# Two attention layers on one core: the order of the work inside a slot, and projections one half per slot

## The reference, cut to what matters

```python
def layer0(x, mask, Wq, Wk, Wv, b):      # batch 8, width 256, 512 tokens, 16 heads of 16
    Q, K, V = (proj(W) for W in (Wq, Wk, Wv))
    att = einsum('bhqd,bhkd->bhqk', Q, K) * (1/4) + b[0]
    att = softmax(att * m + (1 - m) * -1e30, axis=-1)          # m: mask of the keys
    return einsum('bhqk,bhkd->bhqd', att, V), heads joined, transposed
def layer1(x, mask, Wq, Wo):             # 8 heads of 32; queries, keys and values are one projection
    q = xT @ Wq.T
    logits = (scale * q q^T * cmask + (1 - cmask) * -1e30) * rmask
    return (softmax(logits) @ q) @ Wo.T
x = x + layer0(x, cond_2048, ...)
x = x + layer1(x, cond_2048, ...)
x = x + GRU over 128 pairs of steps(cond_2048, x, ...)          # sequential
x = x + last layer(x, ...)
```

## Time and profile before

| | us |
|---|---|
| median of three runs | 2702.07 |
| lowest, highest | 2670.57, 2702.7 |
| the profiled execution's own time | 2684.75 |
| its span, first to last instruction | 2682.5 |
| tensor engine busy (matmuls) | 2099.1, 78% of the span |
| vector engine busy | 1187.9, 44% |
| scalar engine busy | 921.4, 34% |
| pool engine busy | 363.5, 14% |

### The profile page before, as it was taken

One profiled execution on the slowest core, in us unless ns is written; L12 is line 12 of the kernel. 1 busy time (PEld: TensorE's weight loads), 2 busy tenths in 40 slices (PEclk: granted clock), 3 DMA queues, 4 the chain that ended last, 5 costly groups with the idle time before them and its releaser, 6 DMA issues. The chain is left out here.

```text
span 2682.5 us, 89590 instructions
## 1 busy us (share of the span) xinstructions
PE 2099.1 (78%) x37964; PEld 1264.7 (47%) x37964; DVE 1187.9 (44%) x3349; ACT 921.4 (34%) x1836; POOL 363.5 (14%) x996
## 2 busy tenths in 40 slices
PE   4788888888989888967799777777777777777744
PEld 1233333333333433333344666666666666666631
DVE  3455454544445454413001444444444444444456
ACT  0534453434344343432122333333333333333313
POOL 0011111020111111010000111111111111111102
PEclk7889998988898888587899999999999999999967
DMA  7215151505041331211100000000000000000011
GB/s 189 72 59 147 42 137 36 138 27 143 25 134 48 93 81 34 59 55 37 84 0 1 0 0 0 0 0 0 0 0 0 0 0 0 0 0 0 0 36 63
DMA packets 53677, 116.79 MB, mean 44 GB/s; under 512 B 11302, under 2 KB 12198, under 8 KB 49886
## 3 DMA queue, kind: packets, MB, share of 16 engines
q1 hardware_dynamic: 50534, 115.03, 15.3%
q0 software_dynamic: 3072, 0.82, 0.2%
HBM read 77.16 MB, written 37.85 MB: 43 GB/s over the span
## 5 line engine op out<-in xcount | busy, mean ns | idle before, releaser
L789 PE MATMUL gate<-whh,hT 128*8 128x128 f32 x24576 | 718.6, 273 | 136.3 <-POOL xT L687 95.9
L789 PEld LDWEIGHTS gate<-whh,hT 128*8 128x8 f32 x24576 | 644.8, 90 | 168.9 <-POOL xT L687 112.1
L369 DVE TENSOR_REDUCE mx<-MX 128x1 f32<-128x512 f32 x768 | 497.5, 687 | 436.6 <-PE MX L507 434.6
L437 ACT ACTIVATE pr<-ST 128x1024 f32<-128x1024 f32 x384 | 390.2, 1024 | 373.3 <-PE ST L526 372.8
L507 PE MATMUL MX<-K,Q 51*128 51x512 f32 (+1 forms) x768 | 337.8, 558 | 98.0 <-DMA Q<-d_rows 40.9
L751 ACT ACTIVATE act<-pre 128x32 f32<-128x32 f32 x512 | 117.4, 229 | 725.4 <-DVE pre L710 465.8
L507 PEld LDWEIGHTS MX<-K,Q 51*128 51x128 f32 (+1 forms) x768 | 136.2, 215 | 407.3 <-DVE mx L369 205.3
L708 DVE STREAM_TRANSPOSE trn<-gate 128x128 f32<-128x128 f32 x256 | 81.2, 317 | 526.5 <-PE gate L789 526.5
L526 PE MATMUL ST<-Q,K 53*128 53x512 f32 (+1 forms) x768 | 256.6, 510 | 5.4 <-DMA Q<-nmp 4.6
L780 PE MATMUL gate<-identz,giz 128*8 128x32 f32 x8192 | 107.5, 193 | 141.6 <-issue 140.4
L767 PE MATMUL pg<-xT,wih 128*128 128x512 f32 x384 | 167.0, 598 | 19.1 <-DMA identz<-in_ident_dram 19.1
(11 more groups left out here) (124 smaller groups left out, 1696.9 us busy)
## 6 DMA issues: line engine op xcount, KB each, us to landing
d_q<-hi_q SPq DMA_DIRECT2D x32, 256.0 KB
d_q<-lo_q SPq DMA_DIRECT2D x32, 256.0 KB
d_k<-hi_k SPq DMA_DIRECT2D x32, 256.0 KB
d_k<-lo_k SPq DMA_DIRECT2D x32, 256.0 KB
K<-d_k SPq DMA_DIRECT2D x64, 128.0 KB
Q<-d_q SPq DMA_DIRECT2D x64, 128.0 KB
K<-d_k SPq DMA_DIRECT2D x16, 512.0 KB
Q<-d_q SPq DMA_DIRECT2D x16, 512.0 KB
```

The source lines that it names most:

```text
L369: dve.reduce_max(mx[:, u, col:col + 1], banks[0][:, :], AX.X).then_inc(mx_red[u].sem, 1)
L437: act.activation(pr[:, kc % 2, 2 * p:2 * p + 2, :], ST[:, 2 * p * T:(2 * p + 2) * T].rearrange("p (a t) -> p a t", a=2), ACT.Exp, scale=SC ...
L789: last = pe.matmul(ps[g][32 * j:32 * j + B, 0:P], hT[:, u, c, :], whh[:, c, o:o + P], start=c == 0 and g != Z, stop=c == C - 1)
```

## The change

It keeps all banks (2 `MX`, 4 `ST`, `AV`, `DN`) and does the following.

- A slot now reads: score 0, max 0, score 1, max 1, av, (maxT of the unit whose last maxima were in the slot before), score 2, max 2, score 3, max 3, then den and finish where they are due, then one half of a projection. One exponential still covers two heads.
- `LEAD` is 7: the maxima come one slot earlier, and maxT stands in the slot behind the last four of them.
- Projections, values and out go by halves, one in each slot. Only back stays whole.
- The values of layer 1 are no projection any more: `hi` and `lo` of the keys are turned by float32r matmuls with an identity (`ident_r`) and added in PSUM. So layer 1's `x1` is free as soon as its projection is done, and its load waits for that.
- `nm` and `nmp` have two buffers in turn in place of one for each unit; each wait counts all jobs of its kind with one semaphore. `pieces` sends each half when it is there.

```diff
-        LEAD = 6
+        LEAD = 7
...
-            turns = [("max", (u, qb, i), o) for u, qb, o in maxima for i in range(4)]
+            top = [("max", (u, qb, i), o) for i in range(4)]
             pw, pk = divmod((s - 1) % SLOTS, KC)
-            steps = [("score", (w, kc, 0), OFF[w])] + turns[:2] + [("score", (w, kc, 1), OFF[w])]
-            steps += [("av", (pw, pk), OFF[pw] - (1 if s == 0 else 0))] + turns[2:]
-            steps += [("maxT", (u,), o) for u, qb, o in maxima if qb == KC - 1]
-            if s % KC == 1:
-                u = (w - 1) % NU
-                steps.append(("finish", (u,), OFF[u] - (1 if w == 0 else 0)))
-            extra = {0: [("proj", ("k1",), -1)], 2: [("values", (1,), -1), ("back", (1,), -2)], 3: [("out", (), -2)],
-                     4: [("proj", ("q0",), 1)], 5: [("proj", ("k0",), 1)],
-                     17: [("values", (0,), 1)], 18: [("back", (0,), 0)]}
+            st = [("score", (w, kc, i), OFF[w]) for i in range(4)]
+            steps = [st[0], top[0], st[1], top[1], ("av", (pw, pk), OFF[pw] - (1 if s == 0 else 0))]
+            if qb == 0:
+                before = (u - 1) % NU
+                t = KC * before - LEAD + KC
+                steps.append(("maxT", (before,), OFF[before] + (1 if t < 0 else 0)))
+            steps += [st[2], top[2], st[3], top[3]]
+            if kc == 1:
+                before = (w - 1) % NU
+                o = OFF[before] - (1 if w == 0 else 0)
+                if UNITS[before][0] == 1:
+                    steps.append(("den", (before,), o))
+                steps.append(("finish", (before,), o))
+            extra = {0: [("proj", ("k1", 0), -1)], 1: [("proj", ("k1", 1), -1)],
+                     2: [("proj", ("q0", 0), 1)], 3: [("proj", ("q0", 1), 1)],
+                     4: [("proj", ("k0", 0), 1)], 5: [("proj", ("k0", 1), 1)],
+                     6: [("back", (1, 0), -2), ("back", (1, 1), -2)], 7: [("out", (0,), -2)], 8: [("out", (1,), -2)],
+                     9: [("values", (1, 0), -1)], 10: [("values", (1, 1), -1)],
+                     18: [("back", (0, 0), 0), ("back", (0, 1), 0)],
+                     19: [("values", (0, 0), 1)], 20: [("values", (0, 1), 1)]}
...
             for it in range(-1, B + 1):
                 if there(it):
-                    wait(sp, v_mm[1], it - 1, 2)
-                    sp.dma_start(x1[:], x[:, :, it, :]).then_inc(xres_in.sem, 16)
+                    wait(sp, proj_mm, "proj", ("k1", 1), it - 1)
+                    sp.dma_start(x1[:], x[:, :, it, :]).then_inc(xres_in, 16)
...
-            def score(b, banks, w, kc, p):
-                for i in (2 * p, 2 * p + 1):
-                    r, h = head(L, g, i, ROWS[L])
-                    last = pe.matmul(ST[:, i * T:(i + 1) * T], K[r, h, tok(kc)], Q[r, h, :], start=True, stop=True)
-                last.then_inc(st_mm[w].sem, 1)
+            def score(b, bank, w, kc, i):
+                r, h = head(L, g, i, ROWS[L])
+                pe.matmul(ST[i // 2][:, i % 2, :], K[r, h, tok(kc)], Q[r, h, :], start=True, stop=True).then_inc(st_mm, 1)
...
-            def values(b, banks, L):
-                w_, src = (w0[:, 2], xin) if L == 0 else (w1[:, 0], x1)
-                for m in range(2):
-                    walk.clear(m)
-                    for h in range(2):
-                        for k in range(2):
-                            last = pe.matmul(banks[m][:, h * CH:(h + 1) * CH], src[:, k, tok(2 * m + h)], w_[:, k, :], start=k == 0, stop=k == 1)
-                    last.then_inc(v_mm[L].sem, 1)
+            def values(b, bank, L, m):
+                if L == 1:
+                    wait(pe, lo_ev, "proj", ("k1", 1), b)
+                walk.clear()
+                for h in range(2):
+                    if L == 0:
+                        for k in range(2):
+                            last = pe.matmul(bank[:, h * CH:(h + 1) * CH], xin[:, k, tok(2 * m + h)], w0[:, 2, k, :], start=k == 0, stop=k == 1)
+                    else:
+                        for k in range(2):
+                            for half in (hi, lo):
+                                last = pe.matmul(bank[:, h * CH + k * P:h * CH + (k + 1) * P], half["k1"][:, k, tok(2 * m + h)], ident_r[:],
+                                                 start=half is hi, stop=half is lo)
+                last.then_inc(v_mm, 1)
```

More of the change, by code:

```diff
@@ L81, in attention_layers @@
         MX = [pb(f"MX{i}", [P, T]) for i in range(2)]
-        ST = pb("ST", [P, 4 * T])
+        ST = [pb(f"ST{i}", [P, 2, T]) for i in range(2)]
         AV = pb("AV", [P, T])
         DN = pb("DN", [P, T])
[L86 to L96, removed]
@@ L148, in jobs_of @@
[L148 to L165, removed]
@@ new lines, in at_slot @@
+            return steps + extra.get(s, [])
+        PLAN = [step for s in range(SLOTS) for step in at_slot(s)]
+        ORDER = [(name, a, it + o) for it in range(-1, B + 2) for name, a, o in PLAN if there(it + o)]
+        number = {}
+        totals = {}
+        for name, a, b in ORDER:
+            kinds = [name]
+            if name in ("back", "values"):
+                kinds.append((name, a[0]))
+            if name == "av" and a[1] == KC - 1:
+                kinds.append("raw")
+                if UNITS[a[0]][0] == 1:
+                    kinds.append("rawd")
+            for k in kinds:
+                totals[k] = totals.get(k, 0) + 1
+                number[k, a, b] = totals[k]
@@ new lines, in wait, with wait_count, free @@
+        def wait(eng, signal, kind, a, b, per=1):
+            n = number.get((kind, a, b))
+            if n is not None:
+                eng.wait_ge(signal, n * per)
+        def wait_count(eng, signal, n):
+            if n > 0:
+                eng.wait_ge(signal, n)
+        def free(name, a):
+            return {"max": (mx_red, "max"), "maxT": (nm_row, "maxT"), "den": (rden, "finish"), "finish": (yn, "finish"),
+                    "proj": (lo_ev, "proj"), "values": (v_ev, "values"), "out": (xT_sum, "out"),
+                    "back": ((x1_sum, ctx_ev)[a[0]], ("back", a[0])) if name == "back" else None}.get(name)
@@ L187, in run @@
-            def run(self, handlers):
[L188 to L201, removed]
@@ L202, in attention_layers, with clear @@
-        CONST = 6
+                self.eng = eng
+            def clear(self):
+                if self.prior is not None:
+                    signal, kind, a, b = self.prior
+                    wait(self.eng, signal, kind, a, b)
+            def run(self, handlers):
+                users, bank = [None] * len(MX), 0
+                for name, a, b in ORDER:
+                    self.prior = self.bank = None
+                    if free(name, a) is not None:
+                        self.prior, self.bank = users[bank], MX[bank]
+                        users[bank] = (*free(name, a), a, b)
+                        bank = (bank + 1) % len(MX)
+                    if name in handlers:
+                        handlers[name](b, self.bank, *a)
@@ L204, in attention_layers, with rows_sent @@
+        CONST = 7
+        UNIT_AT = {number["maxT", (u,), b]: (u, b) for u in range(NU) for b in range(B)}
+        def rows_sent(eng, n):
+            if n > 0:
+                u, b = UNIT_AT[n]
+                eng.wait_ge(nm_dma[u], 32 * (b + 1))
         block = ctx.enter_context(nc.Block())
@@ L484, in _ @@
             act.wait_ge(const, 48 + CONST)
-            walk = Walk(act)
-            walk.run({"score": score, "av": av, "maxT": max_row, "proj": proj, "values": values, "back": back})
+            Walk(act).run({"score": score, "av": av, "maxT": max_row, "proj": proj, "values": values, "back": back})
         @block.tensor
@@ L566, in proj @@
-            def proj(b, banks, s):
-                w_, src = (w1[:, 0], x1) if s == "k1" else (w0[:, 0 if s == "q0" else 1], xin)
-                wait(pe, *((x1_sum, b, 2) if s == "k1" else (xin_in, b, 32)))
-                for m in range(2):
-                    walk.clear(m)
-                    for k in range(2):
-                        last = pe.matmul(banks[m][:, :], w_[:, k, m * P:(m + 1) * P], src[:, k, :], start=k == 0, stop=k == 1)
-                    last.then_inc(proj_mm[s].sem, 1)
@@ L593, in out_, with den @@
[L593 to L600 removed]
+                last.then_inc(av_mm, 1)
+            def den(b, bank, u):
+                wait(pe, rawd_ev, "rawd", (u, KC - 1), b)
+                walk.clear()
+                for qb in range(KC):
+                    last = pe.matmul(bank[:, 4 * qb:4 * qb + 4], rawd[:, tok(qb)], sel[:], start=True, stop=True)
+                last.then_inc(den_mm, 1)
@@ new lines, in finish, with proj @@
+            def finish(b, bank, u):
+                wait(pe, raw_ev, "raw", (u, KC - 1), b)
+                walk.clear()
+                for qb in range(KC):
+                    last = pe.transpose(bank[:, tok(qb)], raw[:, tok(qb)], ident[:])
+                last.then_inc(fin_mm, 1)
+            def proj(b, bank, s, m):
```

(24 more changed lines are left out.)

371 lines of the change are left out of this document (152 added, 219 removed).

## The result

The changed kernel took 2834.03 us (median of 4 runs, 2827.81 to 2839.65) against 2692.31 for the kernel before beside it. The ratio is 1.054, 95% interval 1.046 to 1.062: slower by 142 us, where 2620 was forecast.

The account below looks back on a forecast made before the run. Bound: the order of the tensor engine's queue, neither engine being full. Terms sum to -5 us an iteration, -33 in all; +15 filling and emptying, -45 clock: -63 from 2684.75 gives 2622, taken as 2620; range 2565 to 2700.

Parts of the forecast that it names:

- the sum's first term: Plain slot of layer 0: stays 3.53 us in the new order, change 0, bounds -0.3 to +0.3.
- a rival at 0.12 and 2662: Broken pairs of scores and maxima bound the slot, the tensor engine being full: 40 us more, 2662; chance 0.12.
- I take two thirds back: -45: Tensor engine's lower clock behind unit ends costs 68 us today; the change regains 45, bounds -68 to +100.
- halves: Projections by halves: 2.8 us a half, 5.6 for two against 4.6 a whole; +2 an iteration, bounds 0 to +5.
- maxT: maxT and finish at unit ends: gain 0.5 us each, 1.1 with denominators; -4.2 an iteration.
- Values of layer 1: Float32r matmuls of 128 columns in place of float32 projection: -1 us an iteration, bounds -1.5 to +4.
- Slots with layer 1's av: Seven slots with layer 1's av and denominators: 0.4 us less each, -3 an iteration.
- Filling and emptying: Work moved at the start and near the end of the attention layers: +15 us together, bounds +6 to +22.
- the 65 us: Time at the lower clock in the seventh iteration, read from a granted clock of 0.75 over 130.7 us.
- The slower rival: Half jobs bring the clock down: ten more slots an iteration at the lower level, 144 us, 2811; chance 0.10.

Follow-up runs that it names:

- e1_pairs: The changed kernel with scores in pairs again in all slots (score 0, score 1, max 0, max 1, av, then likewise 2 and 3): 2644.88 us, 0.986 of before.
- e9: e7 with LEAD 6 and maxT at the end of the slot whose maxima it needs, as before the change: 2700.83 us, 1.004 of before.
- e8: The row probe: the changed kernel plus nine series of 16 products with various row counts behind the attention layers; its total time is not compared.
- e3: e3_whole_jobs: the changed kernel, scores and maxima still alternating, with whole projections, values, back and out in their old slots: 2756.21 us, 1.019 of before.
- e10: e7 with the values of layer 1 computed by projection as before the change: 2654.00 us, 0.988 of before.
- e7: The changed kernel with scores in pairs and whole jobs, spread one kind to a slot: 2607.89 us, 0.972 of before.
- e5: Near the kernel before: LEAD 6, old maxT place, whole jobs, values by projection; but scores and maxima alternate, av earlier, new buffers and semaphores: 2845.89 us, 1.056 of before.
- e11: e7 run once more unchanged, on the same chip as e9 and e10: 2618.88 us, 0.977 of before.

## Why the prediction was wrong

- *"While the banks bound a slot this costs nothing, as summed above"* (of four pairs that become five or six products in a row). This is the step that failed, and the +0 of the sum's first term with it. I counted products and took each at what the earlier trace rows give, where the rows are alike or a pair's first. It was a rival at 0.12 and 2662; the mechanism of broken pairs was right, and its price off: nothing in slots 0 to 8, and where the row count changes twice a head 0.43 a product, eight of them. Of the 0.64 that four such products cost more than in pairs (4 x 0.43 against 1.08, 518.54 to 519.62 in e1_pairs), 0.23 is the score that no longer lies beside the other and 0.41 the two more changes of rows, an estimate from the probe's prices. That fills the engine even at full clock (4.4 for 3.7), so the banks bound nothing any more. A row had warned me: the slot of 5.59 is a full engine already, so that at the lower level nothing could have hidden a longer product.
- *"I take two thirds back: -45"* (the clock). The other failure, and the larger part of the loss. I tied the fall to idle time and small transposes. That is one way (e9 shows it, with most of its 82 us); the other is a run of products with their loads laid open, at an engine that is never idle (slots 9 to 16 and e8, though not slots 17 to 23 of e3). The changed kernel removed the first and brought the second. With pairs the clock comes back: 0.97, 1.00 and 0.96 over an iteration, and 2645 for my 2620, inside the range. That the two are so near is in part luck: the values of layer 1 gave 35 us (e10) and not 7, and the halves cost more than I had.
- *Plain slot, halves, maxT.* The half itself was priced rightly: from the pair at 544.20 to the next maximum, 547.69, are 3.49 (2.2 late for my 2.1), and the second follows 1.14 behind (0.54 late for my 0.7). maxT gains 0.6 a unit at full clock, for my 0.5 (k0 in slot 4 to out in slot 7: 474.85 to 492.52 in e7, 497.56 to 515.87 in e9), and what hung on the clock besides.
- *Values of layer 1.* Taken at 0.12 a matmul with bounds to 0.45, priced at 1.0 saved an iteration; e10 gives 1.6 in their own slots, and 35 us in all with the clock.
- *Slots with layer 1's av.* I credited 3 us an iteration. Slots 17 to 23 took 48.4 for 45.5 in the changed kernel, and 43.9 with pairs. Scores of 99 rows alternate with maxima of 51 there.
- *Filling and emptying.* +15 was forecast; 4 before the first scores, 7 in the stretch around the wait near the end and 8 behind it are 19, with the alternation in the last.
- *Two readings.* A granted clock of 0.75 is half of the way from 1.0 to 0.5, not a quarter; the 65 us are half of 130.7 and right. And 5.59 is a slot with maxima of 97 rows, 3.53 one with 51: against 3.7 in e1_pairs the lower level costs 1.9 a slot, not 2.06.
- *The slower rival* named 2811 by a clock brought down in the slots with halves. The clock came down, but in others, and for another reason: it does so without any half job too (e3, e5). That its time is near the measured one is luck.

The Trainium skill, "TensorE: Matmul & The Clock Gate", Part 3, says that a weight load overlaps a running matmul only when the row groups differ. The probe differs: 53 rows alike, on the same rows, follow each other at 0.23 with a load each, so these loads are hidden; where 53 rows give way to 97, or 99 to 51, it is laid open (0.43). The measurement decides.

## What to carry to other kernels

Before reordering matmuls, write down the number of rows of each and count the changes of the kind measured here, 53 to 97 or 99 to 51: a sequence that alternates so pays about 0.2 us for each product of 512 columns, while 53 beside 51 and 99 beside 97 paid nothing. Where between 53 and 97 rows the price begins was not measured. A tensor engine that is 99% busy can still be at the lower clock (56.45 of 56.70 us at 0.61); read the granted clock slot by slot, not only its idle time. When several parts of a change point different ways, put each back alone: here the order of scores and maxima was worth 189 us and hid a gain of 1.4% in the rest of the change.

## What the runs showed that was not expected

- The clock fell from 1.00 to 0.50 in the middle of 16 products of 53 and 97 rows in turn, 4.6 us in, without idle time (e8). Five series with like rows before it had stayed at 1.00 for 18.3 us. And it stayed at 1.00 through slots 17 to 23 of e3_whole_jobs, where 99 and 51 rows alternate.
- Maxima one slot earlier, so that one 0.3 us transpose (maxT) no longer waits for them at a unit's end, are worth 82 us of 2700 (e9 against e11). Some 0.6 us a unit, 31 in all by an estimate from the slots at full clock, is the wait and what stands around it; the rest came with the clock.
